# Softmax normalised behind the values by a transposed, widened reciprocal instead of on the probabilities by GpSimd

## The chip, the cores and the metric

One NeuronCore of a Trainium2 chip runs the whole program. The metric is the device time of one execution, in microseconds (us). Engines are named as in the profile: PE (TensorE), DVE (VectorE), ACT (ScalarE), POOL (GpSimd), SP (SyncE, which only starts DMAs here).

## What is computed

A decoder layer for 4 sequences of 256 rows and 256 columns in float32: attention (32 query heads on 8 key/value heads of width 64, rotary embedding, causal mask), then a gated state-space scan over a context, then a gated feed-forward network, each behind a layer norm and with its residual. The change lies in the attention:

```
q, k, v = heads of layernorm(x) @ Wq.T, Wk.T, Wv.T       # 32, 8 and 8 heads of 64
q, k    = rope(q), rope(k)
logits  = where(causal, q @ k.T / 8, min)                # each k, v serves 4 query heads
attn    = softmax(logits)
x       = x + concat(attn @ v) @ Wo.T
x       = x + scan of ctx, gated by silu(layernorm(x))   # state y_t, 16 states, 256 channels
x       = x + ffn(layernorm(x))
```

## The kernel before

The attention runs in *units*: one sequence b and one key/value head g, with its 4 query heads; 8 units to a batch (sequence), 32 in all. Batches 1 and 2 are one loop body; the first and the last batch are written out because their order differs. The scan of the state-space layer doesn't depend on the attention: it is cut into 32 steps (one state, one half of the channels, all 1024 positions) which DVE works through between the attention's steps, mostly one a unit. The first batch has none in units 0 to 3 (there DVE prepares the scan, `prepare_scan`, in units 1 to 3, and ACT in units 0 and 1), one in 4 and 5, and two in 6 and 7. The last batch has two in units 5 and 7. Every engine works in the order in which its instructions are written; semaphores tie the engines together.

In iteration g of a batch the engines issue, in this order:

- PE: `scores` of g+1 (twelve products and masks into `ps_s`); at g = 0 the output projection of the batch before (`out_project`, 64 matmuls, L1048); `transpose_p` of g, fills 0 and 1 (L1013, eight transposes into the two banks of `ps_r`), first block of `project` for g+3, fill 2, second block of `project`, `transpose_qk` of g+2 (L941, same banks), `values` of g (L1031, L1035, into `ps_o`).
- ACT: copy of fill 0 (`copy_pt`, L429), the exponentials of g+1 for two of three score banks (L423; each also sums its row into `rsum`), copy of fill 2, the exponentials of the third bank, two copies of the transposed q and k (`copy_qkt`, L408), `copy_attn` of g (L437, `ps_o` to `attn_t`), and the decay of a scan step (L445).
- DVE: `rope` of g+2 (L610 to L616), row maxima of g+1 (`negmax`, L623), copy of fill 1 (L717; in the last batch ACT's), `drive` (L698) and `scan` (L705) of a scan step, `reciprocals` of g+1 (L632), `times_c` (L711, the product with C); a second scan step where there is one; `prepare_scan`. At g = 0 `add_attention` (L727) takes in the output projection of the batch before.
- POOL: `add_rope` of g+2 (L325, L327), `add_y` of the scan steps of iteration g-1 (L347), and `normalise` of g+1 (L335, L339): four multiplies of 128x128 and four of 128x256 by the reciprocal of the row's sum. Rows lie on partitions there, so the factor is one number a partition.

`values` gives its output transposed: head channels on partitions (even head on the lower 64, odd head on the upper), rows along the free axis. A factor by row would be different in every column there.

`out_project` waits on `attn_copied` for the units that it reads. In the last batch it is split: row block 0 of units 0 to 5 in iteration 6, then behind iteration 7 row block 0 of units 6 and 7, row block 1 of units 0 to 5, the transposes of the gated scan, and row block 1 of units 6 and 7.

Of the kernel before, what the change touches and what calls it, by code (L numbers as in the profile page):

```python
# [25 lines left out]
ALU = mybir.AluOpType  # L26
# [3 lines left out]
P = 128  # L30
# [30 lines left out]
def decoder_layer(nc, x, ctx_t, wqkv_t, wo_t, cos_t, sin_t, inproj_t, ssm_par, xproj_t, dtproj_t,  # L61
                  wgate_t, wup_t, wdown_t, s_gate, s_up, s_down, bc_scratch, out):
    ctx = ExitStack()
    with ctx:
# [6 lines left out]

        wqkv = sb("wqkv", [P, KT, KVH, GC])
# [37 lines left out]
        pt = sb("pt", [P, 3, 4 * P])  # L110
        attn_t = sb("attn_t", [P, H // 2, S])
# [18 lines left out]

        flat_n = qkn[:].rearrange("p r t n -> p (r t n)")
# [54 lines left out]
        norm_done = sem("norm_done")  # L186
# [16 lines left out]

        LAST = B - 1
# [72 lines left out]
        def _(pool):  # L277
            pool.sem_inc(norm_done, 1)
# [51 lines left out]
            def normalise(b, g):  # L330
                u = mulof(b, KVH) + g
                pool.wait_ge(consts, 9)
                pool.wait_ge(rinv_done, u + 1)
                for h in range(GRP):
                    nc.gpsimd.tensor_scalar(prob0[:, g % 2, h, :], prob0[:, g % 2, h, :],  # L335
                                            rinv[:, g % 2, h:h + 1], 1.0, ALU.mult, ALU.mult
                                            ).then_inc(norm_done, 1)
                for h in range(GRP):
                    nc.gpsimd.tensor_scalar(prob1[:, g % 2, h, :], prob1[:, g % 2, h, :],  # L339
                                            rinv[:, g % 2, GRP + h:GRP + h + 1], 1.0, ALU.mult, ALU.mult  # L340
                                            ).then_inc(norm_done, 1)

# [9 lines left out]
            normalise(0, 0)  # L352

# [10 lines left out]
            def batch(b, first, last):  # L364
                for g in range(KVH):
# [5 lines left out]
                    if not (last and g + 1 >= KVH):  # L371
                        normalise(b, g + 1)
# [28 lines left out]
        def _(act):  # L401
            def copy_qkt(b, g):
                u = mulof(b, KVH) + g
                slot = g - 2
                for t in range(TB):
                    act.wait_ge(qkt_done, u * 2 + t + 1)
                    bank = (5 * slot + 3 + t) % 2
# [4 lines left out]
            def exps(b, g, part):  # L412
# [4 lines left out]
                for k in range(GRP if part == 0 else 2):  # L417
                    if part == 0:
                        o, i, c = prob0[:, r, k, :], ps_s[:, 0, k * P:(k + 1) * P], k
                    else:  # L420
                        c = GRP + 2 * (part - 1) + k
                        o, i = prob1[:, r, c - GRP, :], ps_s[:, part, k * S:(k + 1) * S]
                    nc.scalar.activation(o, i, ACT.Exp, bias=nmax[:, r, c:c + 1],  # L423
                                         accum_out=rsum[:, r, c:c + 1]).then_inc(exp_done, 1)
# [803 lines left out]
```

## Time and profile before

| | us |
|---|---|
| three runs | 551.68, 553.48, 556.86 |
| median | 553.48 |
| the profiled execution's span | 559.3 |

The span is read off one profiled execution, which lies above the runs' median by 5.8 us; all durations below come from it. Where its time lies:

| stretch of the profiled execution (us) | what runs | length | mean granted clock |
|---|---|---|---|
| 57.5 to 171.6 | first batch's probability transposes on, through its output projection | 114.1 | 0.82 to 1.00 |
| 171.6 to 278.2 | second batch | 106.6 | 0.93 to 1.00 |
| 278.2 to 386.7 | third batch | 108.5 | 0.93 to 1.00 |
| 386.7 to 501.0 | last batch and the turn to the feed-forward part | 114.3 | 0.73 to 1.00 |
| 501.0 to 559.3 | feed-forward part | 58.3 | 0.97 |

The granted clock is the share of TensorE's full 2.4 GHz; in a short stretch it is 1.00 or 0.50 (1.2 GHz), and the means above mix the two. An engine that idles is shown with what ended its idle time; idle time of an engine that nothing waits for costs nothing.

### The profile page before, as it was taken

The numbers are of one execution on the slowest core, as the hardware profiler recorded it, in microseconds if no ns is written. First come the engines' busy times: TensorE is split into PE (matmuls) and PEld (weight loads), VectorE is DVE, ScalarE is ACT, GpSimd is POOL, SyncE is SP. The second block draws the span as 40 slices with busy tenths as digits, with TensorE's granted clock in tenths as the row PEclk, the third lists the DMA queues.
The fourth block names the chain that finished last, engine by engine and source line by source line (L and its number), as shares of the span: only waits on it lengthen the run. The fifth ranks groups of instructions, "written<-read, shape, count | busy, mean of one in ns | idle before, by whom it ended". The sixth has DMA issues, their size and how long they took to land.

```text
span 559.3 us, 8217 instructions
## 1 busy us (share of the span) xinstructions
PE 468.9 (84%) x2568; PEld 321.2 (57%) x2568; DVE 417.4 (75%) x593; ACT 259.9 (46%) x773; POOL 323.2 (58%) x450
## 2 busy tenths in 40 slices
PE   4788988897699898989998988799987975679996
PEld 1433655565487555656865555578654644556674
DVE  3943556898886999989298989872999997655542
ACT  2223874575414564655074544543755654313321
POOL 2823456667976776667466677770679777721000
PEclk9867988898799998989998988999988876999999
DMA  8107400203120102020102021020020110000001
GB/s 318 81 1 209 141 1 0 76 2 127 75 76 2 75 2 76 0 76 5 71 0 75 0 75 50 25 77 0 1 76 21 55 49 27 1 0 1 19 22 35
DMA packets 13710, 28.31 MB, mean 51 GB/s; under 512 B 2824, under 2 KB 8400, under 8 KB 13424
## 3 DMA queue, kind: packets, MB, share of 16 engines
q1 hardware_dynamic: 13120, 27.26, 14.6%
q10 hardware_dynamic: 560, 0.68, 0.3%
q8 instruction: 16, 0.26, 0.2%
q14 instruction: 14, 0.11, 0.1%
HBM read 26.75 MB, written 1.18 MB: 50 GB/s over the span
## 4 chain that ended last, share of the span: by engine, by line
PE 37%; DVE 18%; issue 17%; POOL 17%; ACT 8%; DMA 1%; DVEq 0%; ACTq 0%; POOLq 0%
DVE state L698 10%; POOL prob L335 8%; PE ps_o L1048 7%; PE ps_r L1013 7%; POOL prob L339 6%; PE ps_p L921 6%; ACT prob L423 5%; PE ps_p L1155 4%; PE ps_s L1140 4%; PE ps_s L955 3%; POOL y L347 1%; DMA bc<-ctx_t 1%; DVE nmax L623 1%; PE ps_s L905 1%; ACT pt L429 1%
## 5 line engine op out<-in xcount | busy, mean ns | idle before, releaser
L335 POOL TENSOR_SCALAR prob<-prob,rinv 128x128 f32<-128x128 f32 x128 | 96.3, 770 | 155.3 <-DVE rinv L632 155.2
L429 ACT ACTIVATE pt<-ps_r 128x512 f32<-128x512 f32 x72 | 43.0, 603 | 182.5 <-PE ps_r L1013 182.4
L1013 PE MATMUL ps_r<-ident,prob 128*128 128x128 f32 x384 | 67.0, 323 | 57.7 <-POOL prob L339 57.1
L921 PE MATMUL ps_p<-wqkv,xt 128*128 128x384 f32 x256 | 110.3, 562 | 4.1 <-DVE vv L616 3.2
L423 ACT ACTIVATE prob<-ps_s,nmax 128x256 f32<-128x256 f32 (+1 forms) x256 | 104.7, 437 | 0.0
L698 DVE TENSOR_TENSOR state<-du,bc 128x1024 f32<-128x1024 f32 x32 | 94.2, 2943 | 9.7 <-POOL y L347 9.7
L1013 PEld LDWEIGHTS ps_r<-ident,prob 128*128 128x128 f32 x384 | 54.1, 167 | 78.1 <-issue 37.1
L955 PE MATMUL ps_s<-qkt 64*128 64x256 f32 (+1 forms) x512 | 90.6, 365 | 0.4
L347 POOL TENSOR_TENSOR y<-y,state 128x1024 f32<-128x1024 f32 x32 | 76.2, 2386 | 4.7 <-DVE state L711 4.7
L705 DVE TENSOR_TENSOR_SCAN state<-decay,state 128x1024 f32<-128x1024 f32 x32 | 73.9, 2309 | 1.1
L921 PEld LDWEIGHTS ps_p<-wqkv,xt 128*128 128x128 f32 x256 | 52.8, 228 | 29.6 <-issue 13.4
L955 PEld LDWEIGHTS ps_s<-qkt 64*128 64x128 f32 x512 | 55.3, 192 | 18.0 <-issue 6.5
L623 DVE TENSOR_REDUCE nmax<-ps_s 128x2 f32<-128x512 f32 (+1 forms) x96 | 60.7, 679 | 6.4 <-PE ps_s L966 6.3
L325 POOL TENSOR_TENSOR qkn<-ropec,ropes 128x320 f32<-128x320 f32 x64 | 57.4, 897 | 2.9 <-DVE ropes L612 2.9
L339 POOL TENSOR_SCALAR prob<-prob,rinv 128x256 f32<-128x256 f32 x128 | 59.0, 481 | 0.0
L423 ACT ACTIVATION_READ_ACCUMULATOR prob<-ps_s,nmax 128x1 f32 x256 | 57.4, 224 | 0.0
L1031 PE MATMUL ps_o<-pt,vv 128*64 128x256 f32 x256 | 42.0, 407 | 3.1 <-ACT pt L429 3.1
L1048 PE MATMUL ps_o<-wo,attn_t 128*128 128x256 f32 x192 | 41.9, 379 | 0.0
L445 ACT ACTIVATE decay<-delta,a_neg 128x1020 f32<-128x1020 f32 x32 | 36.2, 1137 | 7.5 <-DVE state L705 4.8
L711 DVE TENSOR_TENSOR state<-state,bc 128x1024 f32<-128x1024 f32 x32 | 39.2, 1225 | 0.2
L1048 PEld LDWEIGHTS ps_o<-wo,attn_t 128*128 128x128 f32 x192 | 36.5, 190 | 4.9
L610 DVE TENSOR_TENSOR ropec<-ps_p,cos_s 128x320 f32<-128x320 f32 x64 | 30.7, 479 | 4.5 <-issue 3.0
(106 smaller groups left out, 573.2 us busy)
## 6 DMA issues: line engine op xcount, KB each, us to landing
bc<-bc_scratch SPq DMA_DIRECT2D x32, 512.0 KB, 4.4
wqkv<-wqkv_t SPq DMA_DIRECT2D x1, 2304.0 KB, 13.6
wo<-wo_t SPq DMA_DIRECT2D x1, 2048.0 KB, 12.6
xs<-x SPq DMA_DIRECT2D x1, 1024.0 KB, 5.9
out<-x SPq DMA_DIRECT2D x4, 256.0 KB, 2.2
wqkv<-wqkv_t SPq DMA_DIRECT2D x1, 768.0 KB, 8.0
wgu_i<-wgate_t SPq DMA_DIRECT2D x1, 704.0 KB, 13.7
wgu_i<-wup_t SPq DMA_DIRECT2D x1, 704.0 KB, 4.7
```

What stands on the lines that cost most here:

```text
L325: nc.gpsimd.tensor_tensor(o[:, 0:ROT], ropec[:, t, :], ropes[:, t, :], ALU.add).then_inc(rope_add, 1)
L335: nc.gpsimd.tensor_scalar(prob0[:, g % 2, h, :], prob0[:, g % 2, h, :], rinv[:, g % 2, h:h + 1], 1.0, ALU.mult, ALU.mult).then_inc(norm_do ...
L339: nc.gpsimd.tensor_scalar(prob1[:, g % 2, h, :], prob1[:, g % 2, h, :], rinv[:, g % 2, GRP + h:GRP + h + 1], 1.0, ALU.mult, ALU.mult).then ...
L347: nc.gpsimd.tensor_tensor(y[:, g % 2, :], y[:, g % 2, :], state[:, g % 2, :], ALU.add).then_inc(state_free, 1)
L423: nc.scalar.activation(o, i, ACT.Exp, bias=nmax[:, r, c:c + 1], accum_out=rsum[:, r, c:c + 1]).then_inc(exp_done, 1)
L623: nc.vector.tensor_reduce(nmax[:, g % 2, c:c + k], ps_s[:, part, :].rearrange("p (k s) -> p k s", k=k), AX.X, ALU.max, negate=True).then_i ...
L698: nc.vector.tensor_tensor(state[:, g % 2, :], du[:, g % 2, :], bc[:, r, 0, :], ALU.mult).then_inc(drive_done, 1)
L705: nc.vector.tensor_tensor_scan(state[:, g % 2, :], decay[:, g % 2, :], state[:, g % 2, :], 0.0, ALU.mult, ALU.add).then_inc(decay_free, 1)
L921: last = nc.tensor.matmul(ps_p[:, t, 0:GC], xt[:, k, t * P:(t + 1) * P], wqkv[:, k, gg, :], start=(k == 0), stop=(k == KT - 1))
L955: return nc.tensor.matmul(ps_s[:, bank, col:col + keys], qkt[lo:lo + HD, r, h // 2, t * P:(t + 1) * P], qkt[lo:lo + HD, r, 2, 0:keys], sta ...
L1013: last = nc.tensor.transpose(ps_r[:, bank, k * P:(k + 1) * P], src, ident[:])
L1048: last = nc.tensor.matmul(o, attn_t[:, k, t * P:(t + 1) * P], wo[:, k, :], start=(k == 0), stop=(k == H // 2 - 1))
```

## The change

The probabilities stay unnormalised. `normalise` and its semaphore go. The exponentials write their sums into `rsum` in another order (the four row sums of one row block beside each other, in head order), and `reciprocals` inverts them as before. ACT then widens the eight reciprocals to 8 x 64 columns (`widen`); four PE transposes of 128x128 (`replicate`) turn them so that partition p holds the factor of p's head and the free axis runs over rows, which is the layout of `ps_o`; ACT copies that to `rep_s` (two buffers), and DVE multiplies the values' output by it on the way to `attn_t` (`scale_attn`), where ACT copied before (`copy_attn`). The `ps_r` banks are assigned anew: fills 0 and 2 and the second qk block use bank 0; fill 1, the first qk block and the replica use bank 1. `rwide` lies in a part of `x1` that is free until the last batch's residual.

```diff
+        rep_s = sb("rep_s", [P, 2, 4 * P])
...
+        rwide = x1[:, LAST * TB:B * TB, :].rearrange("p t n -> p (t n)").rearrange("p (c k) -> p c k", k=HD)
...
-            def normalise(b, g):
-                u = mulof(b, KVH) + g
-                pool.wait_ge(consts, 9)
-                pool.wait_ge(rinv_done, u + 1)
-                for h in range(GRP):
-                    nc.gpsimd.tensor_scalar(prob0[:, g % 2, h, :], prob0[:, g % 2, h, :],
-                                            rinv[:, g % 2, h:h + 1], 1.0, ALU.mult, ALU.mult
-                                            ).then_inc(norm_done, 1)
...
-                    if not (last and g + 1 >= KVH):
-                        normalise(b, g + 1)
...
-            def copy_attn(b, g):
...
+            def widen(b, g):
+
+                u = mulof(b, KVH) + g
+                act.wait_ge(rinv_done, u + 1)
+                if not (isinstance(b, int) and 8 * b + g < 1):
+                    act.wait_ge(rep_done, u)
+                nc.scalar.activation(rwide[:], rinv[:, g % 2, :].rearrange("p (c k) -> p c k", k=1).to_broadcast(
+                    [P, 2 * GRP, HD]), ACT.Copy).then_inc(wide_done, 1)
+
+            def copy_rep(b, g):
+
+                u = mulof(b, KVH) + g
+                act.wait_ge(rep_done, u + 1)
+                if not (isinstance(b, int) and 8 * b + g < 2):
+                    act.wait_ge(attn_copied, u)
+                nc.scalar.activation(rep_s[:, g % 2, :], ps_r[:, 1, :], ACT.Copy).then_inc(rep_copied, 1)
...
                 for g in range(KVH):
                     copy_pt(b, g, 0)
+                    widen(b, g)
...
                         copy_qkt(b, g + 2)
-                    copy_attn(b, g)
+                    copy_rep(b, g)
...
+            def scale_attn(b, g):
+
+                u = mulof(b, KVH) + g
+                dve.wait_ge(pv_done, u + 1)
+                dve.wait_ge(rep_copied, u + 1)
+                if g == 0 and not (isinstance(b, int) and b == 0):
+                    dve.wait_ge(wo_done, b + 1)
+                nc.vector.tensor_tensor(attn_t[:, 2 * g:2 * g + 2, :], ps_o[:].rearrange("p (k s) -> p k s", k=2),
+                                        rep_s[:, g % 2, :].rearrange("p (k s) -> p k s", k=2), ALU.mult
+                                        ).then_inc(attn_copied, 1)
...
                         times_c(*v)
+                    scale_attn(b, g)
                     if first and g < 4:
                         prepare_scan(g)
...
                 if 0 in fills:
-                    pe.wait_ge(norm_done, u * 8 + 9)
+                    pe.wait_ge(exp_done, u * 8 + 8)
...
+                    elif not first:
+                        pe.wait_ge(rep_copied, u)
...
+            def replicate(b, g, qk_after):
+
+                u = mulof(b, KVH) + g
+                pe.wait_ge(wide_done, u + 1)
+                if qk_after:
+                    pe.wait_ge(qkt_copied, u * 2 + 5)
+                else:
+                    pe.wait_ge(pt_1, u + 2)
+                for pair in range(GRP // 2):
+                    for t in range(TB):
+                        c = t * GRP + 2 * pair
+                        src = rwide[:, c:c + 2, :].rearrange("p o k -> p (o k)")
+                        last = nc.tensor.transpose(ps_r[:, 1, pair * S + t * P:pair * S + (t + 1) * P],
+                                                   src, ident[:])
+                last.then_inc(rep_done, 1)
...
                     if not (last and g + 2 >= KVH):
                         transpose_qk(b, g + 2)
+                    replicate(b, g, not (last and g + 2 >= KVH))
                     values(b, g)
```

## Rows read from the trace of the kernel before

**Rows 1.** The page's first part: busy time, share of the span and instructions.
```profile
PE 468.9 (84%) x2568; PEld 321.2 (57%) x2568; DVE 417.4 (75%) x593; ACT 259.9 (46%) x773; POOL 323.2 (58%) x450
```

**Rows 2.** List of waits: engine, line, releaser, total us, times, longest.
```profile
PE ps_r L1013 <- POOL prob L339: 57.1, 26, 5.3
```

**Rows 3.** Timeline, one middle unit: start, us, engine, line, operation, idle before.
```profile
283.73 2.28 POOL L335 TENSOR_SCALAR prob<-prob,rinv 128x128 f32<-128x128 f32 x4 [11.98 <-DVE rinv L632]
...
284.64 0.48 DVE L610 TENSOR_TENSOR ropec<-ps_p,cos_s 128x320 f32<-128x320 f32 x1
...
285.99 1.85 POOL L339 TENSOR_SCALAR prob<-prob,rinv 128x256 f32<-128x256 f32 x4
...
286.50 1.93 DVE L623 TENSOR_REDUCE nmax<-ps_s 128x2 f32<-128x512 f32 x3
...
287.96 1.09 PE L1013 MATMUL ps_r<-ident,prob 128*128 128x128 f32 x8 [0.27 <-POOL prob L339]
...
289.09 0.69 DVE L717 COPY pt<-ps_r 128x512 f32<-128x512 f32 x1 [0.66 <-PE ps_r L1013]
...
289.70 3.73 DVE L698 TENSOR_TENSOR state<-du,bc 128x1024 f32<-128x1024 f32 x1
...
289.99 2.36 POOL L347 TENSOR_TENSOR y<-y,state 128x1024 f32<-128x1024 f32 x1
...
295.67 0.17 DVE L632 RECIPROCAL rinv<-rsum 128x8 f32<-128x8 f32 x1
```

**Rows 4.** Timeline of the same unit, ACT and PE.
```profile
288.65 0.60 ACT L429 ACTIVATE pt<-ps_r 128x512 f32<-128x512 f32 x1 [2.49 <-PE ps_r L1013]
...
289.15 0.47 ACT L423 ACTIVATE prob<-ps_s,nmax 128x256 f32<-128x256 f32 x1
...
292.66 0.65 PE L1031 MATMUL ps_o<-pt,vv 128*64 128x256 f32 x4
...
292.79 0.93 ACT L408 ACTIVATE qkt<-ps_r 128x384 f32<-128x384 f32 x2
...
294.11 1.14 PE L955 MATMUL ps_s<-qkt 64*128 64x128 f32 x8
```

**Rows 5.** Stretches: us, busy time of each engine, granted clock, DMA share, GB/s.
```profile
181.16:193.45 12.29, 9.51 (x62) 6.33 (x62) 11.60 (x15) 6.70 (x22) 8.62 (x14) 1.00 0.15 57
193.45:205.73 12.28, 11.19 (x62) 7.27 (x62) 11.54 (x15) 6.81 (x22) 8.61 (x14) 0.86 0.08 31
...
255.10:278.20 23.10, 23.10 (x125) 18.53 (x126) 11.94 (x15) 6.70 (x22) 12.97 (x18) 1.00 0.13 46
278.20:288.00 9.80, 9.53 (x63) 6.31 (x61) 9.34 (x15) 6.71 (x22) 4.27 (x9) 1.00 0.00 0
```

**Rows 6.** Groups by line: busy us, mean ns, idle before and its releaser.
```profile
L698 DVE TENSOR_TENSOR state<-du,bc 128x1024 f32<-128x1024 f32 x32 | 94.2, 2943 | 9.7 <-POOL y L347 9.7
...
L727 DVE TENSOR_TENSOR x<-ps_o,xs 128x512 f32 (+1 forms) x3 | 2.1, 690 | 28.7 <-PE ps_o L1048 28.7
```

**Rows 7.** Timeline, the drive of the middle batch's unit 0.
```profile
279.93 1.22 DVE L698 TENSOR_TENSOR state<-du,bc 128x1024 f32<-128x1024 f32 x1
```

**Rows 8.** Timeline, the first batch's last preparation and its end.
```profile
99.21 1.18 DVE L679 TENSOR_TENSOR y<-y,decay 128x1024 f32<-128x1024 f32 x1
...
103.75 0.06 DVE L689 MEMSET decay<- 128x4 f32 x1
...
154.44 1.14 PE L955 MATMUL ps_s<-qkt 64*128 64x128 f32 x8
...
157.63 13.98 PE L1048 MATMUL ps_o<-wo,attn_t 128*128 128x256 f32 x64
...
161.37 1.23 DVE L711 TENSOR_TENSOR state<-state,bc 128x1024 f32<-128x1024 f32 x1
```

**Rows 9.** Timeline, the end of the last batch's attention.
```profile
487.17 7.14 PE L1048 MATMUL ps_p<-wo,attn_t 128*128 128x256 f32 x32 [0.78 <-ACT attn_t L437]
...
489.99 1.22 DVE L711 TENSOR_TENSOR state<-state,bc 128x1024 f32<-128x1024 f32 x1
```

More of the change, by code:

```diff
@@ L351, in _ @@
             add_rope(0, 1)
-            normalise(0, 0)
             def x1_rstd(lo, hi, step):
@@ L403, in copy_qkt @@
                 u = mulof(b, KVH) + g
-                slot = g - 2
                 for t in range(TB):
                     act.wait_ge(qkt_done, u * 2 + t + 1)
-                    bank = (5 * slot + 3 + t) % 2
+                    bank = (1 + t) % 2
                     nc.scalar.activation(qkt[:, g % 2, :, t * P:(t + 1) * P],
@@ L428, in copy_pt @@
                 act.wait_ge(pt_done, u * 3 + fill + 1)
[L429 removed]
+                nc.scalar.activation(pt[:, fill, :], ps_r[:, fill % 2, :], ACT.Copy
                                      ).then_inc(pt_1 if fill == 1 else pt_act, 1)
[L432 removed]
+            def widen(b, g):
                 u = mulof(b, KVH) + g
[L434 to L439 removed]
+                act.wait_ge(rinv_done, u + 1)
[9 more added lines that the diff above has]
+                nc.scalar.activation(rep_s[:, g % 2, :], ps_r[:, 1, :], ACT.Copy).then_inc(rep_copied, 1)
             def decays(b, g):
@@ L926, in transpose_qk @@
                 u = mulof(b, KVH) + g
-                slot = g - 2
+                ahead = not isinstance(b, int) or KVH * b + g >= 2
                 for t in range(TB):
                     pe.wait_ge(rope_add, u * 4 + 2 * (t + 1))
-                    bank = (5 * slot + 3 + t) % 2
+                    bank = (1 + t) % 2
                     if t == 0:
@@ L993, in transpose_p @@
                 r = g % 2
+                first = isinstance(b, int) and KVH * b + g < 1
                 if 0 in fills:
-                    pe.wait_ge(norm_done, u * 8 + 9)
+                    pe.wait_ge(exp_done, u * 8 + 8)
                 for fill in fills:
-                    bank = (5 * g + fill) % 2
                     if fill == 2:
                         pe.wait_ge(pt_act, u * 2 + 2)
-                    elif qk_before:
-                        pe.wait_ge(qkt_copied, u * 2 + 3 + fill)
+                    elif fill == 0 and qk_before:
+                        pe.wait_ge(qkt_copied, u * 2 + 4)
                     elif fill == 0:
-                        pe.wait_ge(pt_1, u + 1)
+                        pe.wait_ge(pt_act, u * 2 + 1)
+                    elif not first:
+                        pe.wait_ge(rep_copied, u)
                     else:
-                        pe.wait_ge(pt_act, u * 2 + 1)
+                        pe.wait_ge(dt_v, 2 * EB)
                     for k in range(4):
@@ L1012, in transpose_p @@
                             src = prob1[:, r, place[k], P:S]
-                        last = nc.tensor.transpose(ps_r[:, bank, k * P:(k + 1) * P], src, ident[:])
+                        last = nc.tensor.transpose(ps_r[:, fill % 2, k * P:(k + 1) * P], src, ident[:])
                     last.then_inc(pt_done, 1)
+            def replicate(b, g, qk_after):
[12 more added lines that the diff above has]
+                last.then_inc(rep_done, 1)
             def values(b, g):
@@ L1124, in transpose_x2 @@
                     pe.wait_ge(x2lo_done, b)
+                else:
+                    pe.wait_ge(rep_copied, UNITS)
                 for k in range(KT):
```

31 lines of the change are left out of this document (10 added, 21 removed).

## The prediction

> **What bounds the kernel now.** I read four views. The page's busy shares come first [rows 1]: PE is busiest at 84%, DVE 75%, POOL 58%, so no engine is full and the bound must be a ring of waits. The wait list names it [rows 2]: PE's probability transposes wait 57.1 us in all for POOL's normalisation, 26 times. Third, the timeline of one middle unit [rows 3]. Follow one turn: the reciprocal releases POOL at 283.73; its eight multiplies end at 285.99 + 1.85 = 287.84; PE transposes at 287.96; DVE copies at 289.09, drives the scan at 289.70, scans, and writes the next reciprocal at 295.67. That is 12.29 us a turn, and DVE idles only 0.66 of it. PE had finished its scores and idles up to 2.8 us. The drive is the other thing to see: 3.73 us beside POOL's y addition (289.99 to 292.35), 1.22 us with POOL silent [rows 3, 7]: the two engines take turns. Fourth, ACT and PE of the same unit [rows 4], a path that has slack today and will not have it afterwards. The middle batches have 12 such interior steps (units 1 to 7, twice six), each about 12.28 us [rows 5].
>
> I call T the start of a unit's probability transposes (287.96 above).
>
> **What is removed.** Eight POOL multiplies a unit, 2.28 + 1.85 = 4.1 us [rows 3], and with them POOL's link in the ring. The transposes now wait for the exponentials, long done. Also ACT's attention copy, which hung behind the values.
>
> **What is added, a unit.** (1) ACT widens the reciprocals, 128x512. No row has ACT copy that from SBUF; lower bound nothing, upper 0.6, nearest the 0.60 PSUM copy whose successor starts 0.50 later [rows 4]: I take 0.50. It sits between the first copy and the exponentials, so it is on ACT's path. (2) Four PE transposes, half of the eight that took 1.09 [rows 3]: 0.55; low clock 1.0. (3) ACT's copy of the replica, 0.50, behind the qk copies, where the old attention copy was; hidden under the values. (4) DVE's product, PSUM times SBUF, 128x512: the 0.69 of the same form [rows 6], 0.65 as a step. It is last in DVE's turn.
>
> **What is moved, and the new wait.** The replica's transposes share bank 1 with the first qk block, so PE must wait for ACT's first qk copy, which ACT issues only after all eight exponentials. Values and next scores queue behind that wait in PE's order. Today the values start at T + 4.70 while ACT still works on the exponentials; ACT's lateness costs nothing. Afterwards the ring is, from [rows 4]: 0.69 to the first copy, 0.50 copy, 0.50 widen, 3.64 eight exponentials with the copy between them (289.15 to 292.79), 0.53 first qk copy (half of its pair, plus its tail), 0.10 handover, 0.55 replica, 1.45 values (292.66 to 294.11), 3.19 scores (154.44 to 157.63 [rows 8]): 11.15 us. DVE's turn must fit in it: today's 12.29 less 0.66 idle and the drive of 3.73 leaves 7.9; with a drive of 2.1 and the new product 0.65 it is 10.65. The drive is 2.1 because POOL starts on rope's results where it now normalises. Its second rope addition ends 1.2 after rope (half of 8.62 - 4.13 - 2.36 [rows 3, 5], with its start), its y addition 2.36 later, 3.55 after rope; the drive can start 1.9 (maxima) + 0.65 (copy) = 2.55 after rope and needs 1.1 once POOL is silent: 1.0 + 1.1. So the ring sets the pace, 11.15, with 0.45 to spare.
>
> **The clock.** The unit at 181.16 kept 1.00 of the clock and needed 9.51 us of PE; its successor, whose transposes came after the longest pause, had 0.86 and needed 11.19 [rows 5]: a fall from 2.4 to 1.2 GHz costs 1.7 us of PE, today inside PE's slack. Of the new ring about half is PE, so a fall would cost 0.9. The new pause before the replica is about 1.2 us (qk transposes end near T + 4.75, ACT releases at T + 5.95). I allow a fall in one unit of four: 11.4 us; with a fall in every unit it would be 12.05. The Trainium skill (TensorE: Matmul & The Clock Gate, section "A second HAM failure mode: psum-queue depth-cycling") warns that small idles between groups of matmuls, in a kernel that cycles through PSUM banks, make the clock swing between its levels, which is this pattern; taken fully, it would bring the higher of these two figures. The trace agrees in part: every second unit has the fall, behind the longer pause.
>
> **Sum, against the profiled 559.3 us.**
> Interior steps: 12 x (11.4 - 12.28) = -10.6.
> Edge steps of the two middle batches: from unit 0 to 1 POOL was no bound (9.80 in [rows 5]), so each grows to 11.15: with the exact starts +1.4, twice +2.9. From unit 7 across the output projection: 23.1 [rows 5] becomes 7.95 (T to end of values) + 3.19 + 13.8 = 24.95, +1.8; the other such step already ran at a lower clock, +0.2. Together +4.9.
> First batch: here DVE prepares the scan after its turn in units 1 to 3. Before, that began at the reciprocal; now the product with the replica stands first, waits for the values' end (2.3 us behind it by the ring's terms), and costs 0.65. A turn becomes product 0.65, preparation 4.6 (99.21 to 103.8 [rows 8]), rope 1.86, first of three maxima 0.62 [rows 3], exponentials and copy 3.64, qk copy and handover 0.63, replica 0.55, values 1.45 = 14.0, about as long as today, but now PE's low clock is in it. Unit 1 starts 1.9 late (11.15 against today's POOL-free 9.3), its preparation 1.9 + 2.3 + 0.65, some 4.5 to 5 late, and so the last preparation, which ended at 103.8 [rows 8], ends near 109.2, with low clock 110.5. Then DVE is the bound: the 58.8 us from 103.8 to its last product with C at 162.6 [rows 8] shrink to 54.3 (four turns of 10.2, 11.5, 15.1 and 17.5, built as the 10.65 above with none, one or two steps of the scan more and the two odd jobs; POOL's multiplies no longer cross the drives), so DVE, with one product more, ends at 164 to 165. That was harmless before: the output projection began at 157.63 while DVE still scanned. Now its last operand is DVE's product behind both scans: it starts 6.4 to 7.5 late, and PE, having paused, adds up to 1.9 at low clock. I take +8.5.
> Last batch: DVE-bound. Drives cost 2.94 on average, 1.22 alone [rows 6, 7]: POOL freed saves about 0.9 in each of ten, and some 4 us of waits behind it, less 8 x 0.65 for the products: DVE's last product with C, done at 491.2 [rows 9], comes 8 us earlier. But PE's 32 matmuls of the projection (7.14 from 487.17) no longer overlap it: they wait for DVE's product. 491.2 - 8 + 0.65 + 7.14 + 1.9 (clock) = 492.9 against 494.3 today. I take -2, counting some less of the clock.
> Sum: -10.6 + 4.9 + 8.5 - 2 = +0.8, a profile near 560. The profiled span lies 5.8 us above the median of the runs, 553.48; the difference carried over gives **554.3 us**.
>
> **Rivals.** *Nothing lost to the clock (faster):* interior 11.15 (-13.6), first batch +5, last -6: -9.7, 543.8 us. For it: pauses of 1.2 us; against: two long new pauses of PE at the batches' ends. Chance 0.22. *PE alone sets the pace (faster):* if ACT could release the replica early, a unit is PE's 9.5 + 0.55; 12 x -2.2 and the edges give some 30 less, 524 us. Against it stands the order of ACT's queue. 0.03. *The clock falls in the pause of every unit (slower):* ring 12.05, interior -2.8, edges +6.7, first batch +10, last 0: +14, 567.5 us. It decides from two units in three on. Today half of the interior units have a fall [rows 5], but behind pauses of up to 2.8 us, over twice the new one. 0.2. (This is the rule of the Trainium skill's page named above.) *DVE becomes the bound (slower):* if the drive still collides fully, 3.73 for 2.1, DVE's turn is 12.3 and the interior gain is gone: +11.4, 565 us. It decides from a drive of 2.6 on; POOL's earlier release speaks against. 0.13. *The forecast, gain and loss cancel:* 0.42; its own range 548 to 560.
>
> **How the numbers follow.** About 1% (5.5 us) is what a measurement here can tell from no change. The faster cases hold 0.25, the cancelling one 0.42, the slower 0.33. The range, 544 to 568, takes in the cases next to the forecast; the widening's bounds (0 to 0.6 a unit, -6 to +1.2 us in all) and the replica's low-clock price lie inside.
>
> **What would show it.** Right: interior steps near 11.4 us; PE's replica waiting on ACT's qk copy; drives near 2.1; the first output projection starting near 164 behind a wait for DVE's product; the first batch longer, the middle ones shorter. Wrong: interior steps at 10 or at 12.3 and more; half clock in most units; no wait of PE at the first projection; the qk copies early in ACT's queue.

## The result and the profile after

| | before | after |
|---|---|---|
| median of 18 runs each (lowest to highest), us | 559.45 (551.68 to 561.74) | 561.84 (557.0 to 562.91) |
| ratio, 95% interval | 1 | 1.0125 [1.0098, 1.0152] |
| span of the profiled execution, us | 559.3 | 560.1 |

The change made the kernel slower, by 1.2% in the ratio and by 0.4% in the medians, where 554.3 us was forecast. The ratio is formed from the fast runs of each kernel alone and the medians from all 18, so the two can differ. When the kernel before was timed against itself later, the ratio came out at 0.9929 [0.9866, 0.9993] with medians of 559.3 and 559.96 us; the changed kernel's repetition gave 1.005 [1.0011, 1.009] with medians of 562.02 and 559.55. So the readings of the loss run from 0.4% to 1.2%, and its sign is surer than its size.

Lines moved: the probability transposes are L1019 now (L1013 before), the output projection L1070 (L1048), the drive L691 (L698), the scan L698 (L705), the y addition L334 (L347). New: the widening L422, the replica's transposes L1034 and its copy L431, DVE's product L719.

The page's first part after the change, to be set beside [rows 1]:

```profile
PE 469.9 (84%) x2696; PEld 322.1 (58%) x2696; DVE 415.5 (74%) x625; ACT 274.2 (49%) x805; POOL 170.9 (31%) x194
```

POOL lost half of its work (323.2 to 170.9 us), ACT gained 14 us, DVE did 32 products more in less time. Nothing of this says faster or slower. The list of waits does (engine, line, releaser, total us, times, longest):

```profile
PE ps_r L1034 <- ACT qkt L390: 35.2, 30, 1.3
...
PE ps_o L1070 <- DVE attn_t L719: 7.6, 1, 7.6
```

The 57.1 us of [rows 2] are gone. In their place stand 30 short waits of the replica for ACT's copy of q and k, and one of 7.6 us in which the first output projection waits for DVE's product. Timeline of a middle unit, which answers to [rows 3] and [rows 4]:

```profile
226.77 1.04 PE L1019 MATMUL ps_r<-ident,prob 128*128 128x128 f32 x8
227.41 0.60 ACT L413 ACTIVATE pt<-ps_r 128x512 f32<-128x512 f32 x1 [3.55 <-PE ps_r L1019]
227.53 2.36 POOL L334 TENSOR_TENSOR y<-y,state 128x1024 f32<-128x1024 f32 x1
...
227.90 0.62 ACT L422 ACTIVATE x<-rinv 128x512 f32<-128x512 f32 x1
...
228.42 0.47 ACT L407 ACTIVATE prob<-ps_s,nmax 128x256 f32<-128x256 f32 x1
...
228.55 2.43 DVE L691 TENSOR_TENSOR state<-du,bc 128x1024 f32<-128x1024 f32 x1
...
232.06 0.93 ACT L390 ACTIVATE qkt<-ps_r 128x384 f32<-128x384 f32 x2
...
232.66 0.66 PE L1034 MATMUL ps_r<-ident,x 128*128 128x128 f32 x4 [1.17 <-ACT qkt L390]
233.25 0.65 PE L1053 MATMUL ps_o<-pt,vv 128*64 128x256 f32 x4
...
234.70 1.14 PE L960 MATMUL ps_s<-qkt 64*128 64x128 f32 x8
234.82 0.69 DVE L719 TENSOR_TENSOR attn_t<-ps_o,rep_s 128x512 f32<-128x512 f32 x1 [0.26 <-PE ps_o L1057]
...
237.90 1.04 PE L1019 MATMUL ps_r<-ident,prob 128*128 128x128 f32 x8
```

This is the ring of the forecast, link by link: copy, widening, exponentials, the first half of the qk copies, replica, values, scores. 237.90 - 226.77 = 11.13 us. The stretches of the changed kernel, in the columns of [rows 5]: one interior step, then six in a row in each middle batch.

```profile
204.53:215.65 11.12, 9.95 (x66) 6.73 (x65) 10.84 (x17) 7.21 (x23) 4.55 (x6) 1.00 0.09 33
193.40:260.14 66.74, 59.74 (x391) 40.37 (x390) 65.30 (x93) 43.25 (x138) 27.32 (x31) 1.00 0.14 49
...
296.20:362.93 66.73, 59.73 (x392) 40.36 (x391) 65.27 (x93) 43.26 (x138) 27.30 (x31) 1.00 0.15 47
```

All twelve steps are alike, 11.12 us at a granted clock of 1.00. Before, ten of them took about 12.28 and one in each batch 12.53; the twelve together are 14.4 us shorter now. The loss is where the first batch ends. First the order of its unit starts (PE, changed kernel):

```profile
57.00 1.04 PE L1019 MATMUL ps_r<-ident,prob 128*128 128x128 f32 x8
...
68.25 1.04 PE L1019 MATMUL ps_r<-ident,prob 128*128 128x128 f32 x8
...
79.43 1.04 PE L1019 MATMUL ps_r<-ident,prob 128*128 128x128 f32 x8
...
94.26 1.04 PE L1019 MATMUL ps_r<-ident,prob 128*128 128x128 f32 x8
...
144.30 1.04 PE L1019 MATMUL ps_r<-ident,prob 128*128 128x128 f32 x8
...
166.74 15.71 PE L1070 MATMUL ps_o<-wo,attn_t 128*128 128x256 f32 x64 [7.60 <-DVE attn_t L719]
182.29 1.04 PE L1019 MATMUL ps_r<-ident,prob 128*128 128x128 f32 x8
```

The projection began at 157.63 before and took 13.98 [rows 8]. And DVE and POOL just ahead of it:

```profile
158.12 1.23 DVE L704 TENSOR_TENSOR state<-state,bc 128x1024 f32<-128x1024 f32 x1
159.26 1.22 DVE L691 TENSOR_TENSOR state<-du,bc 128x1024 f32<-128x1024 f32 x1
...
159.43 3.25 POOL L334 TENSOR_TENSOR y<-y,state 128x1024 f32<-128x1024 f32 x1 [4.75 <-DVE state L704]
...
160.52 4.31 DVE L698 TENSOR_TENSOR_SCAN state<-decay,state 128x1024 f32<-128x1024 f32 x1
...
164.86 1.23 DVE L704 TENSOR_TENSOR state<-state,bc 128x1024 f32<-128x1024 f32 x1
...
166.00 0.68 DVE L719 TENSOR_TENSOR attn_t<-ps_o,rep_s 128x512 f32<-128x512 f32 x1
```

PE waits for the product at 166.00, which stands in DVE's order behind a whole second scan step, and that step's scan took 4.31 us, not 2.29.

The profiled executions differ before the changed code begins. Up to the first probability transposes (the start of the first of them is T0 below) PE does the same work in all kernels and waits at its end for none of the changed parts. This took between 50.9 and 57.5 us in the profiles of this study, at different granted clocks. So profiles are compared from T0 to the end of the span: 501.8 us before (559.3 - 57.49) and 503.1 after (560.1 - 57.00), 1.3 us more.

| stretch, between starts of probability transposes | before | after | difference |
|---|---|---|---|
| first batch | 113.96 | 125.29 | +11.3 |
| second batch | 106.79 | 102.78 | -4.0 |
| third batch | 108.46 | 102.79 | -5.7 |
| last batch, to the last 8 matmuls of its projection | 108.2 | 107.4 | -0.8 |
| rest | 64.4 | 64.8 | +0.4 |

### The profile page after: what moved, and what is told of

It is laid out like the page before. It is cut to its first block, busy times and chain, and to the rows that moved or that the text cites. A ratio compares the mean times of both kernels' runs of the same rounds, so it can differ in the third digit from the quotient of the medians.

```text
span 560.1 us, 8372 instructions
## 1 busy us (share of the span) xinstructions
PE 469.9 (84%) x2696; PEld 322.1 (58%) x2696; DVE 415.5 (74%) x625; ACT 274.2 (49%) x805; POOL 170.9 (31%) x194
## 3 DMA queue, kind: packets, MB, share of 16 engines
HBM read 26.75 MB, written 1.18 MB: 50 GB/s over the span
## 4 chain that ended last, share of the span: by engine, by line
PE 50%; ACT 23%; DVE 14%; issue 8%; POOL 3%; DMA 1%; ACTq 0%; DVEq 0%; POOLq 0%
ACT prob L407 14%; PE ps_s L960 11%; PE ps_o L1070 8%; PE ps_o L1053 6%; PE ps_p L1179 4%; PE ps_s L971 3%; DVE state L698 3%; PE ps_r L1034 3%; ACT pt L413 3%; DVE state L691 3%; PE ps_s L1164 2%; PE ps_o L1057 2%; ACT x L422 2%; PE ps_p L1070 2%; PE ps_r L1019 2%
## 5 line engine op out<-in xcount | busy, mean ns | idle before, releaser
L926 PE MATMUL ps_p<-wqkv,xt 128*128 128x384 f32 x256 | 98.9, 513 | 11.7 <-DVE vv L609 10.6
L334 POOL TENSOR_TENSOR y<-y,state 128x1024 f32<-128x1024 f32 x32 | 78.1, 2441 | 26.0 <-DVE state L704 26.0
L698 DVE TENSOR_TENSOR_SCAN state<-decay,state 128x1024 f32<-128x1024 f32 x32 | 79.4, 2482 | 1.1
L691 DVE TENSOR_TENSOR state<-du,bc 128x1024 f32<-128x1024 f32 x32 | 70.5, 2204 | 1.3 <-POOL y L334 1.3
L926 PEld LDWEIGHTS ps_p<-wqkv,xt 128*128 128x128 f32 x256 | 46.1, 200 | 34.0 <-DVE ropes L605 12.4
L407 ACT ACTIVATION_READ_ACCUMULATOR prob<-ps_s,nmax 128x1 f32 x256 | 58.9, 230 | 0.0
L1019 PE MATMUL ps_r<-ident,prob 128*128 128x128 f32 x384 | 53.0, 275 | 0.8 <-ACT pt L413 0.8
L1019 PEld LDWEIGHTS ps_r<-ident,prob 128*128 128x128 f32 x384 | 46.0, 142 | 13.2 <-issue 5.4
L1034 PE MATMUL ps_r<-ident,x 128*128 128x128 f32 x128 | 21.0, 288 | 36.1 <-ACT qkt L390 35.2
L1070 PE MATMUL ps_o<-wo,attn_t 128*128 128x256 f32 x192 | 43.7, 390 | 7.6 <-DVE attn_t L719 7.6
L1070 PEld LDWEIGHTS ps_o<-wo,attn_t 128*128 128x128 f32 x192 | 37.6, 197 | 13.2 <-DVE attn_t L719 7.9
L437 ACT ACTIVATE decay<-delta,a_neg 128x1020 f32<-128x1020 f32 x32 | 36.2, 1143 | 12.6 <-DVE state L698 6.7
L1034 PEld LDWEIGHTS ps_r<-ident,x 128*128 128x128 f32 x128 | 13.7, 143 | 43.3 <-ACT qkt L390 22.5
L719 DVE TENSOR_TENSOR attn_t<-ps_o,rep_s 128x512 f32<-128x512 f32 x32 | 22.1, 690 | 18.9 <-PE ps_o L1057 18.7
## 6 DMA issues: line engine op xcount, KB each, us to landing
wqkv<-wqkv_t SPq DMA_DIRECT2D x1, 2304.0 KB, 13.7
```

The source lines that it names most:

```text
L334: nc.gpsimd.tensor_tensor(y[:, g % 2, :], y[:, g % 2, :], state[:, g % 2, :], ALU.add).then_inc(state_free, 1)
L691: nc.vector.tensor_tensor(state[:, g % 2, :], du[:, g % 2, :], bc[:, r, 0, :], ALU.mult).then_inc(drive_done, 1)
L698: nc.vector.tensor_tensor_scan(state[:, g % 2, :], decay[:, g % 2, :], state[:, g % 2, :], 0.0, ALU.mult, ALU.add).then_inc(decay_free, 1)
L926: last = nc.tensor.matmul(ps_p[:, t, 0:GC], xt[:, k, t * P:(t + 1) * P], wqkv[:, k, gg, :], start=(k == 0), stop=(k == KT - 1))
L1019: last = nc.tensor.transpose(ps_r[:, fill % 2, k * P:(k + 1) * P], src, ident[:])
L1070: last = nc.tensor.matmul(o, attn_t[:, k, t * P:(t + 1) * P], wo[:, k, :], start=(k == 0), stop=(k == H // 2 - 1))
```

## The experiments

The theory when they were planned: the transposed factor itself is cheap (0.5 us here and there); what eats the gain is three positions in in-order queues, the product behind both scan steps on DVE, the replica ahead of the values on PE, the widening ahead of the exponentials on ACT. The rival: the work itself is what costs, and the positions are worth little. Each of the first experiments moves one thing. Ratios are to the kernel before. The changed kernel was profiled twice, at 503.1 and 502.3 us from T0; the gains from T0 below are against 503.1, so each is uncertain by about 1 us.

### The kernel before, again

Unchanged. It asks whether the interior steps of before (12.28) are a habit or an accident of one profile.

> The kernel before, unchanged, as a second look. Its runs spread from 551.7 to 561.7 us, and the profile of it that the forecast used (span 559.3 us) may be one of the slow ones. Theory of the base: a look that falls near 553 us shows the same 12.28 us steps between units of the middle batches (they are set by VectorE and GpSimd, not by TensorE's clock), and the 6 us less lie in the first and the last batch and in the projections, where TensorE is on the path and its clock fell. Rival: the 12.28 us steps themselves vary, by half a microsecond each. If the look is again at 559 to 561 us it tells nothing apart and its ratio should be 1.00.

Measured: 559.3 us, ratio 0.9929 [0.9866, 0.9993]; span 557.7, from T0 500.3. Interior steps 12.27 and 12.28 again, once 12.52. The base of the forecast's interior term holds. That the ratio of a kernel to itself can come out 0.7% off, with medians 0.1% apart, bounds what the ratios below can say.

### The changed kernel, again

> The kernel after, unchanged, once more beside before on this chip, because the identical kernel before was measured at 0.993 of itself (interval 0.987 to 0.999): what is the change worth? Theory (profiles: 559.3 before, 557.7 before again, 560.1 after): the two are within 1% of each other, ratio 1.00 to 1.01, and the profile repeats steps of 11.12 us and a first projection near 166.7. Rival: the first comparison's 1.0125 holds, ratio 1.01 to 1.015.

Measured: 562.02 us, ratio 1.005 [1.0011, 1.009]; span 558.4, from T0 502.3. Interior steps 11.13 again, the first projection from 164.51 for 16.44 us. From T0 the profile repeats within 0.8 us. Inside the first batch less repeats: its third step is 13.21 us here and 14.83 there, where the granted clock was 0.50 from 88.2 to 91.6.

### DVE's product ahead of the second scan step

```diff
                     if units:
                         times_c(*units[0])
+                    scale_attn(b, g)
                     for v in units[1:]:
                         drive(*v)
                         scan(*v)
                         times_c(*v)
-                    scale_attn(b, g)
```

> After, with one thing moved: in iterations with two steps of the scan DVE multiplies the values' output (scale_attn) before the second step, not behind it. Theory of order: the first output projection, which waited 7.6 us for that product, starts about 7 us earlier, and the last projection's 32 matmuls about 4 us earlier, with less of the half clock: 9 to 11 us less than after, some 551 us, ratio to before 0.985 to 0.995. Rival, that the loss is TensorE's added work and its clock and not who stands behind whom: no more than 2 us less, ratio 1.01.

Measured: 548.46 us, ratio 0.9813 [0.9725, 0.9902]; span 548.7, from T0 491.55, which is 11.5 less than the changed kernel's 503.1. DVE, POOL and PE at the end of the first batch, in the timeline:

```profile
159.41 0.68 DVE L719 TENSOR_TENSOR attn_t<-ps_o,rep_s 128x512 f32<-128x512 f32 x1
159.57 2.35 POOL L334 TENSOR_TENSOR y<-y,state 128x1024 f32<-128x1024 f32 x1 [4.74 <-DVE state L704]
160.01 2.99 DVE L691 TENSOR_TENSOR state<-du,bc 128x1024 f32<-128x1024 f32 x1
160.15 15.67 PE L1070 MATMUL ps_o<-wo,attn_t 128*128 128x256 f32 x64 [1.18 <-DVE attn_t L719]
163.03 2.29 DVE L698 TENSOR_TENSOR_SCAN state<-decay,state 128x1024 f32<-128x1024 f32 x1
```

The product is out at 160.09, the wait is 1.18 and not 7.60, and the second scan step runs beside the projection as it did before the change. One line in another place turns a loss into a gain of 1.9% [1.0, 2.8], a little more than the 9 to 11 us expected. Of the 11.5 us, 6.8 lie in the first batch and 4.8 in the last batch with what follows. So the queue position, not the product, cost these 11 us. The long scan is gone as well: the y addition now falls beside the drive, which takes 2.99, and the scan is back at 2.29.

### The values ahead of the replica

```diff
-                    replicate(b, g, not (last and g + 2 >= KVH))
                     values(b, g)
+                    replicate(b, g, not (last and g + 2 >= KVH))
```

> After, with one thing moved: TensorE issues the values of a unit before the four transposes of the widened reciprocals, not behind them, so the values no longer wait for ACT's copy of q and k. Theory (the ring of 11.12 us runs through that wait): the values fill TensorE's pause of 1.2 us, the ring shortens to about 9.95 us and VectorE's turn of 10.7 us becomes the bound: 12 interior steps at 10.7 instead of 11.12 (-5), the steps at the batches' edges -1 each (-4), the first batch a little: 8 to 12 us less than after, ratio to before 0.99. Rival, that TensorE is simply full (9.95 us busy of 11.12): steps stay above 11.0 and the time changes by less than 2 us.

Measured: 548.97 us, ratio 0.9849 [0.9769, 0.9929]; span 547.2, from T0 491.8, 11.3 less. The steps of the second batch and what fills them:

```profile
190.67:200.56 9.89, 9.73 (x65) 6.73 (x66) 9.86 (x14) 7.21 (x23) 3.81 (x5) 1.00 0.01 2
200.56:210.47 9.91, 9.76 (x64) 6.72 (x65) 9.88 (x14) 7.24 (x23) 4.56 (x5) 1.00 0.29 107
```

A PE step is 9.9 us three times, then 10.8 to 11.1. In the two shown PE waits for nothing (its only pause is 0.16 of issue), so 9.9 us is PE's own pace. DVE is busy for all but 0.03, with 14 instructions where a whole turn has 17: its turn, from reciprocal to reciprocal, takes 10.78 already. PE runs ahead for three units and then goes at DVE's pace. The values no longer wait for ACT's qk copy, and the ring through ACT is off the critical path; DVE is next. The gain lies in the middle batches, 4.8 us in each, and behind them, 1.8; the first batch gains nothing. The first projection still waits (from 165.30, for 15.65): this edit doesn't touch that loss.

### The scan's preparation ahead of the product

```diff
-                    scale_attn(b, g)
                     if first and g < 4:
                         prepare_scan(g)
+                    scale_attn(b, g)
```

> After, with one thing moved: in units 0 to 3 of the first batch DVE prepares the scan before it multiplies the values' output, as it did in the kernel before. Theory of order: the preparation starts at the reciprocal again, 2.9 us earlier in each of units 1 to 3; a turn there falls from 14.0 to 11.5 us, VectorE's chain through the first batch ends 6 to 7 us earlier and with it the first output projection: 5 to 7 us less than after, ratio to before 1.00. Rival, that TensorE's ring of 11.1 us and its clock limit the first batch: 0 to 2 us less.

Measured: 554.91 us, ratio 0.9919 [0.9876, 0.9961]; span 553.2, from T0 496.25, 6.9 less. PE's unit starts in the first batch:

```profile
79.38 1.04 PE L1019 MATMUL ps_r<-ident,prob 128*128 128x128 f32 x8 [0.16 <-issue]
...
91.99 1.04 PE L1019 MATMUL ps_r<-ident,prob 128*128 128x128 f32 x8 [0.16 <-issue]
...
103.42 1.04 PE L1019 MATMUL ps_r<-ident,prob 128*128 128x128 f32 x8 [0.16 <-issue]
...
114.85 1.04 PE L1019 MATMUL ps_r<-ident,prob 128*128 128x128 f32 x8 [0.16 <-issue]
```

Steps of 12.6, 11.4 and 11.4 us, where the changed kernel has 14.8, 13.5 and 14.2. The forecast's reading, that the preparation stands behind a product which waits for the end of the values, is confirmed, with 6.9 us at stake in three units (6.1 against the repetition of the changed kernel).

### The three orders together

> After with the three moves that each gained alone: the product ahead of the second scan step (13 us less than after), the values ahead of the replica (13 less), the preparation ahead of the product (7 less). Theory of order: in the first batch they add up nearly fully, in the middle the steps stay at VectorE's 10.8 us: 22 to 28 us less than after, 534 to 540 us, ratio to before 0.955 to 0.965. Rival: they all relieve the same wait (the first projection), so together no more than 16 us less, 546 us.

Measured: 527.74 us, ratio 0.9455 [0.9367, 0.9543]; span 523.5, from T0 468.6. That is 34.5 less than the changed kernel, where 22 to 28 were expected; the three alone sum to 29.7. The middle batches add up (9.6 us); what exceeds the sum lies in the first batch, 17.3 us against 13.7, and behind the third. Why was not tried. The first projection begins at 148.94 behind a pause of 0.25 and takes 14.08. One step of the second batch:

```profile
203.32:214.11 10.79, 10.36 (x64) 6.68 (x65) 10.76 (x17) 7.33 (x23) 4.55 (x5) 1.00 0.26 97
```

DVE is busy 10.76 of 10.79 us. As in the kernel with the values ahead, DVE's turn of 10.78 and no ring of waits sets the step. PE is close behind: its first three steps here take 9.9 as well.

### The widening at the end of ACT's turn

```diff
+            widen(0, 0)
...
                     copy_pt(b, g, 0)
-                    widen(b, g)
...
                     copy_rep(b, g)
+                    if not (last and g + 1 >= KVH):
+                        widen(b, g + 1)
```

> After, with one thing moved: ACT widens the reciprocals of the next unit at the end of its turn, where it idles, and not between the first copy and the exponentials. This prices the widening on ACT's path, which the forecast took as 0.50 us of the ring. Theory: the ring falls from 11.12 to 10.62 us, where VectorE's turn of 10.7 takes over: interior steps 10.7 to 10.8, 4 to 8 us less than after in all. Rival, that the widening hides under the wait for the row maxima or costs less than 0.2: steps stay above 10.95.

Measured: 548.59 us, ratio 0.982 [0.9742, 0.9898]; span 545.1, from T0 493.4, 9.7 less, where 4 to 8 were expected. The unit starts 196.22, 206.83, 217.45, 228.06 are 10.61 apart, 0.51 less than 11.12: the widening's place on the ring was worth what it held ACT's next instruction back, and the replica's wait for the qk copy shrank with it:

```profile
212.22 0.66 PE L1036 MATMUL ps_r<-ident,x 128*128 128x128 f32 x4 [0.67 <-ACT qkt L390]
```

### The four together

All edits above in one kernel.

> all_three with the widening moved to the end of ACT's turn as well. Theory: the middle steps are VectorE's already (10.8 us) and gain nothing, the steps at the batches' edges (9.9 us) and the first batch, where ACT's path counts, gain 0.3 to 0.5 each: 3 to 6 us less than all_three, 522 to 525 us, ratio to before 0.935 to 0.94. Rival: it is all VectorE's by now, 0 to 1 us less. Either way it should be far faster than before and after.

Measured: 525.86 us, ratio 0.9449 [0.938, 0.9517]; span 521.3, from T0 470.3 against 468.6 for the three. The rival came true: the earlier widening adds nothing once the ring through ACT is slack. The two kernels can't be told apart.

### The kernel before without its normalisation

```diff
-            normalise(0, 0)
...
-                    if not (last and g + 1 >= KVH):
-                        normalise(b, g + 1)
...
-                if not (isinstance(b, int) and 8 * b + g < 2):
-                    dve.wait_ge(norm_done, u * 8 - 7)
...
-                    pe.wait_ge(norm_done, u * 8 + 9)
+                    pe.wait_ge(exp_done, u * 8 + 8)
```

> The kernel before without the normalisation and with nothing in its place: GpSimd's eight multiplies a unit and the waits on them are left out, so the output lacks the division by the row sums. It measures what the removed part alone was worth, so that the cost of the added parts is after minus this. Theory: without the link through GpSimd, VectorE's turn (12.29 less 0.66 idle less 1.6 of the drive) sets the pace: interior steps 10.0 to 10.1 (-27), the batches' edges unchanged, first and last batch some 5 to 10 less each: 515 to 528 us, ratio 0.93 to 0.945. Then the added parts cost 33 to 45 us. Rival, that TensorE's matmuls and the clock were the limit all along: not under 545 us.

This kernel leaves out the division by the row sums, so its output is not the layer's.

Measured: 500.14 us, ratio 0.8963 [0.8887, 0.904]; span 496.7, from T0 444.2. The removal alone is worth 501.8 - 444.2 = 57.6 us, far more than the 33 to 45 expected. Two steps of it:

```profile
191.69:201.88 10.19, 9.59 (x60) 6.24 (x61) 10.16 (x15) 6.81 (x22) 4.55 (x5) 1.00 0.33 105
246.58:255.87 9.29, 9.13 (x62) 6.33 (x62) 8.88 (x14) 6.70 (x22) 1.85 (x3) 1.00 0.00 0
```

The first batch's steps fall to 9.3 to 10.9 as well and its projection begins at 140.61. So the parts that the change adds cost 503.1 - 444.2 = 58.9 us. The removal was half of the change and was seen; the other half ate it whole. It can be split by order and work: with the three orders together 468.6 - 444.2 = 24.4 us are left. So 34.5 of the 58.9 us were order, and 24.4 are what the added work still costs in that order.

### The same, with the values' output moved by DVE

The kernel above, but with the copy of `ps_o` to `attn_t` on DVE at the end of its turn, where the product stands after the change, and no replica.

```diff
@@ ACT, behind copy_qkt
-                    copy_attn(b, g)
...
@@ DVE, last of its turn
+                    copy_attn(b, g)
...
+                nc.vector.tensor_copy(attn_t[:, 2 * g:2 * g + 2, :], ps_o[:].rearrange("p (k s) -> p k s", k=2)
+                                      ).then_inc(attn_copied, 1)
```

> The kernel before without the normalisation (the division by the row sums is left out, as in no_normalise), and with one part of the change: the values' output is moved to attn_t by DVE, at the end of its turn, instead of by ACT. It splits the 59 us that the added parts cost (after against no_normalise, both from the first probability transposes on: 503.1 and 444.2 us) into the step on DVE and the replica's path. Theory: the step costs its place in DVE's order, the first projection and the preparation above all, 20 to 30 us, and 0.65 us in each interior step, where DVE is the bound (10.2 becomes 10.8): from the first transposes on 465 to 475 us, ratio to before 0.92 to 0.94. Rival: the replica (ACT's two operations, TensorE's wait and four transposes) is the larger part, and this costs less than 15 us, ratio 0.92 or less.

Measured: 538.0 us, ratio 0.9635 [0.9518, 0.9751]; span 536.5, from T0 479.0. That is 34.8 us over the kernel without normalisation, where 20 to 30 were expected, for 32 instructions that keep DVE busy for 21.9 us: 15.3 us in the first batch, 9.5 in the two middle ones, 9.9 in the rest. Two of the 17 executions of the kernel before that were timed beside this one took 2378 us; why is not known, and they are in no ratio. The first projection shows the rest (from 158.01, after a pause of 8.40, for 16.92):

```profile
158.01 16.92 PE L1042 MATMUL ps_o<-wo,attn_t 128*128 128x256 f32 x64 [8.40 <-DVE attn_t L709]
```

So of the 58.9 us, 34.8 come with moving the values' output on DVE, its work and its place together, and the remaining 24.1 with the widening, the replica and the wait for bank 1. That this is near the 24.4 above is chance: the two cuts divide the cost differently.

### POOL's y addition behind DVE's second scan

```diff
-            def add_y(b, g):
+            def add_y(b, g, behind=0):
                 u = mulof(b, KVH) + g
+                if behind:
+                    pool.wait_ge(hc_done, u + 1 + behind)
```

`behind` is 1 for the first of two scan steps of a unit, else 0.

> After, with one wait added on GpSimd: where DVE does two steps of the scan in a row, GpSimd adds the first step's y only when the second step is done (first batch, units 6 and 7; last batch, unit 5; not the last unit). In after the freed GpSimd starts that addition at once and DVE's second scan takes 4.3 us instead of 2.3, in three places. Theory (the two engines take turns at two-input operations in SBUF, and this is a term that the forecast lacked): two of the three scans fall to 2.3, the first projection starts 2 us earlier, 2 to 4 us less than after, ratio to before 1.00. Rival: the 4.3 us come from something else, and nothing changes or it gets slower by the added wait.

Measured: 559.76 us, ratio 1.0073 [1.0026, 1.0121]; span 551.6, from T0 500.7, 1.6 to 2.4 less than the changed kernel's two profiles. The scan by line, in the changed kernel:

```profile
L698 DVE TENSOR_TENSOR_SCAN state<-decay,state 128x1024 f32<-128x1024 f32 x32 | 79.4, 2482 | 1.1
```

and here, then in the kernel before:

```profile
L701 DVE TENSOR_TENSOR_SCAN state<-decay,state 128x1024 f32<-128x1024 f32 x32 | 75.4, 2355 | 1.1
```

```profile
L705 DVE TENSOR_TENSOR_SCAN state<-decay,state 128x1024 f32<-128x1024 f32 x32 | 73.9, 2309 | 1.1
```

Two of the three long scans are back at 2.3 us with POOL held off them. The collision is real and worth about 2 us, at the lower end of the 2 to 4 expected. In the ratio it can't be seen; it rests on the traces.

## Why the forecast failed, step by step

- **Ring, interior steps.** Forecast 11.15 at full clock, 11.4 with a fall in one unit of four; measured 11.12, twelve times. The links were right: the widening takes 0.62 and its successor starts 0.52 later (0.50 forecast), the replica 0.66, a step of 0.59 (0.55), its wait 1.17 (1.2). The allowance for the clock was not needed: -14.4 us in place of -10.6, half a microsecond of it because one step in each batch had taken 12.53 before and not 12.28. This term was mis-sized. The Trainium skill (TensorE: Matmul & The Clock Gate, section "A second HAM failure mode: psum-queue depth-cycling") has small idles between groups of matmuls make the clock swing; the trace does not agree here, with twelve pauses of 1.17 us, 11.12 us apart, at 1.00 throughout.
- **DVE's turn.** Forecast 10.65; DVE is busy 10.84 us in the step shown. The drive still meets the y addition: 2.43 in that unit, 2204 ns over all 32, where 2.1 was forecast and 2943 measured before [rows 6]. It fits in the ring with 0.28 to spare, and the rival in which DVE is the bound did not come true, but it was nearer than thought. With the values ahead of the replica, where the ring is shorter, it is what comes next.
- **Edge steps.** From unit 0 to 1 11.12 (9.71 before), across the projection 24.93 (24.95 forecast). The step held.
- **First batch.** This term was mis-sized: +8.5 forecast, +10.8 at the start of the second batch (182.29 against 171.45), +11.3 from T0. The mechanism was the one named: preparation behind product behind values, then the projection behind product behind scans. The experiments with the preparation and the product moved ahead show both. The projection began at 166.74, not 164 to 165. What was missed is that a POOL without multiplies begins its y addition as soon as the first scan step is through, beside DVE's second one: 2.0 us on the scan. I had counted the multiplies' end as a pure gain for DVE. Before, it was POOL that paid there. In the timeline of the kernel before, the four small multiplies (2.28 in [rows 3]) took 6.30, and the drive and the scan beside them, 1.22 and 2.29, lost nothing:

```profile
156.88 6.30 POOL L335 TENSOR_SCALAR prob<-prob,rinv 128x128 f32<-128x128 f32 x4 [3.67 <-DVE rinv L632]
157.79 1.22 DVE L698 TENSOR_TENSOR state<-du,bc 128x1024 f32<-128x1024 f32 x1
159.05 2.29 DVE L705 TENSOR_TENSOR_SCAN state<-decay,state 128x1024 f32<-128x1024 f32 x1
```

- **Last batch.** -2 forecast, -0.8 measured. The same collision strikes in units 5 and 7 there (two scans of 4.3 us), and the waiting projection took longer than 7.14 + 1.9:

```profile
484.85 10.15 PE L1070 MATMUL ps_p<-wo,attn_t 128*128 128x256 f32 x32 [4.75 <-DVE attn_t L719]
```

- **The sum.** In the table's terms the middle batches gave -9.7 (forecast -10.6 + 4.9 = -5.7), the first +11.3 (+8.5), the last with what follows -0.4 (-2): +1.2 from T0 where +0.8 was forecast. It is so near by luck, because errors cancel: 4.0 us too little gain, against 2.8 too little loss and 1.6 too much gain.
- **The base.** This is the step that failed. The profiled execution's 559.3 us lay 5.8 above the median of three runs, and I subtracted that difference: 553.48 + 0.8. Over 18 runs the median before is 559.45, so the three runs had come from the lower part of the spread, and 6.0 of the 7.5 us by which the forecast missed are this. A span and a run's time aren't the same measure either: the changed kernel's profiled execution has a span of 560.1 and a time of 561.87, and every other run on record shows 1.7 to 1.9 us between the two. So the profiled execution of before was one of about 561.1 us, near the top of its spread. From 559.45 the same sum gives 560.3 against 561.84 measured. These 1.5 us are left, and how much of the measured 1.2% is the change and how much the spread of runs, stays open: from T0, the two profiles of after lie 0.5 and 1.3 us above the 501.8 of before, and the second profile of before 1.5 below it.
- **What was not asked.** The sum of parts was nearly right, and yet hid that it was made of 57.6 us gained and 58.9 lost. The rival of PE alone setting the pace (0.03, 524 us) did not come true with this order of instructions. With the three orders together the same change runs at 527.74, where DVE sets most steps and PE three in each middle batch.

## What to carry to other kernels

When an operation moves to another engine, price its place in that engine's queue as well as its duration: here 21.9 us of copies cost 34.8, and three reorderings that remove no work gave back 34.5. Put the product that another engine waits for ahead of work that nobody waits for soon. And take more than three runs as the base before a forecast of one per cent: three had erred by 6 us against 18.

## What the runs showed of the hardware

- **DVE and POOL on SBUF operands.** Of a DVE instruction with two SBUF inputs and a POOL instruction, the one that comes second waits for the first. The drive takes 1.22 alone and 3.73 in [rows 3]; the scan 2.29 alone and 4.31; the y addition 2.36 alone and 3.25 when it starts into a drive that is running (159.43 above). POOL's multiplies, with one tensor input, wait as well (156.88 above), though they cost DVE nothing there. The drive of [rows 3] starts 0.29 before the y addition and pays nonetheless. It came while POOL was in a row of additions without a pause, and its end, 293.43, is 1.08 behind the end of the y addition, 292.35. POOL just before the y addition, in the kernel before:

```profile
288.89 0.87 POOL L325 TENSOR_TENSOR qkn<-ropec,ropes 128x320 f32<-128x320 f32 x1
289.71 0.33 POOL L327 TENSOR_TENSOR qkn<-ropec,ropes 128x64 f32<-128x64 f32 x1
```

  DVE products with one input in PSUM kept their times beside POOL's additions (0.48 for rope, 0.68 for L719 at 159.41 of the kernel with the product ahead). The Trainium skill (GPSIMD Engine Reference, section "1. Specifications") states that POOL shares its SBUF interfaces with VectorE, with contention for DVE instructions that have two SBUF inputs; the trace agrees, and gives the size: up to three times the duration.
- **The clock and short pauses.** With 1.17 us in every 11.12 it stayed at 1.00. In the kernel with the product ahead pauses of 2.68 (before 148.17), of 1.26 (before the replica at 153.92) and of 1.18 (before the projection at 160.15) follow each other, and the projection began at half speed, 1.2 GHz. Stretches of that kernel, and then of the changed one, where the last pause was 7.60:

```profile
160.15:163.60 3.45, 3.45 (x9) 2.79 (x10) 3.42 (x2) 0.00 (x0) 1.76 (x1) 0.53 0.00 0
163.60:170.00 6.40, 6.40 (x31) 5.65 (x30) 6.37 (x11) 0.00 (x0) 2.45 (x5) 1.00 0.33 113
```

```profile
159.90:166.70 6.80, 0.00 (x0) 0.00 (x0) 6.73 (x5) 0.00 (x0) 2.78 (x1) 0.50 0.00 0
166.50:170.00 3.50, 3.26 (x8) 2.64 (x9) 3.50 (x10) 0.00 (x0) 2.35 (x5) 0.50 0.82 268
```

  In the changed kernel PE stands still from 159.14 on, behind pauses of 2.68 and 1.26 as well, and the granted clock is down from 159.9 on: it fell at about the same point in both kernels, 0.8 us into the long pause and so not for its length. The projection took 15.67 and 15.71 us, against 13.98 in [rows 8] with no pause and 14.08 with the three orders together and a pause of 0.25. The price was 1.7 us in both. It was more in other profiles: 16.44 behind 7.65 in the changed kernel's repetition, 16.92 behind 8.40 with the copies on DVE. Which of PE's earlier activity decides was not settled.
- **The opening.** The same instructions up to T0 took 50.9 to 57.5 us in different profiles, more than most effects studied here. Its cause, beyond that the granted clock differed, was not tried.
